# The router of a two-layer mixture kernel: kern products first, copies dropped, three of eight x pairs loaded transposed

## The reference, cut to what matters

```python
h = gelu(gelu(embedding @ W0 + b0) @ W1 + b1)
att = softmax(h @ W2 + b2)                                  # 32 x 8
agg_w = einsum('bk,koi->boi', att, weight[..., 0])
out = einsum('boi,bih->boh', agg_w, x) + (att @ bias_k)[:, :, None]
logits = einsum('bsh,he->bse', out, gate_w)
topv, topi = top_k(logits, 2); w = softmax(topv)
x = x + einsum('bsh,eho,bse->bso', out, expert_w, w_e)
```

## Time and profile before

| | us |
|---|---|
| runs, median of three (lowest, highest) | 869.05 (866.9, 869.88) |
| the profiled execution, its time | 863.12 |
| its span, first to last instruction | 861.3 |
| PE busy (x4356) | 824.4, 96% |
| DVE busy | 407.4, 47% |
| ACT busy | 229.6, 27% |
| POOL busy | 107.4, 12% |

### The profile page before, as it was taken

The page is one execution under the profiler, slowest core; times in us unless marked ns, Lnnn a source line. Parts: engine busy times, 40 slices in busy tenths (PEclk is TensorE's granted clock), DMA queues, the critical chain, the costliest instruction groups (busy, mean ns, idle before and its releaser), DMA issues.

```text
span 861.3 us, 13429 instructions
## 1 busy us (share of the span) xinstructions
PE 824.4 (96%) x4356; PEld 680.6 (79%) x4357; DVE 407.4 (47%) x944; ACT 229.6 (27%) x359; POOL 107.4 (12%) x145
## 2 busy tenths in 40 slices
PE   6999679999999999999999999999999999999986
PEld 5565468888888888888888888888898889889863
DVE  1577753142333313333133051466666656656597
ACT  2565333142333313333243151310010010001100
POOL 1122221101101001111011112121112111100000
PEclk9999879999999999999999999999999999999999
DMA  8744359655372724727246243575644654630048
GB/s 265 311 170 151 120 210 404 267 179 200 120 257 73 285 92 134 244 78 287 85 157 226 92 167 117 194 242 133 153 105 106 157 127 97 141 78 24 1 127 263
DMA packets 60789, 142.98 MB, mean 166 GB/s; under 512 B 6832, under 2 KB 23488, under 8 KB 60608
## 3 DMA queue, kind: packets, MB, share of 16 engines
q1 hardware_dynamic: 40096, 87.12, 31.1%
q0 software_dynamic: 9968, 36.19, 14.5%
q10 hardware_dynamic: 10704, 19.41, 6.0%
HBM read 94.45 MB, written 39.85 MB: 156 GB/s over the span
## 4 chain that ended last, share of the span: by engine, by line
PE 83%; DVE 6%; DMA 4%; issue 3%; ACT 1%; SPq 1%; DVEq 0%; ACTq 0%; POOL 0%; POOLq 0%
PE bank L1269 62%; PE bank L1308 6%; PE bank L1260 4%; PE bank L1317 4%; PE bank L1169 2%; PE bank L1371 1%; PE bank L1137 1%; DVE work L1111 1%; PE bank L1148 1%; DMA work<-in_expert_w 1%; PE bank L1192 1%; PE bank L1217 1%; DVE rank_all L812 1%; DMA work<-y_scratch,pos_c 1%; DMA x1p<-res 1%
## 5 line engine op out<-in xcount | busy, mean ns | idle before, releaser
L1269 PE MATMUL bank<-weights,l_hi 128*128 128x512 f32 x1696 | 523.6, 390 | 0.0
L1269 PEld LDWEIGHTS bank<-weights,l_hi 128*128 128x128 f32 x1696 | 319.2, 188 | 64.7
L1269 PE MATMUL bank<-weights,l_lo 128*128 128x512 f32 x848 | 335.8, 396 | 1.2 <-DVE l_lo L900 1.1
L1269 PEld LDWEIGHTS bank<-weights,l_lo 128*128 128x128 f32 x848 | 159.7, 188 | 33.4 <-issue 2.3
L900 DVE TENSOR_TENSOR l_lo<-bank,l_hi 128x512 fp32r<-128x512 f32 x37 | 25.6, 693 | 183.6 <-ACT l_hi L679 183.6
L932 DVE TENSOR_TENSOR weights<-work,weights 128x1024 fp32r<-128x1024 f32 x64 | 76.2, 1223 | 50.4 <-ACT weights L690 49.8
L690 ACT ACTIVATE weights<-work 128x1024 fp32r<-128x1024 f32 x64 | 65.1, 1054 | 41.3 <-DMA work<-in_expert_w 23.2
L537 POOL DMA_INDIRECT work<-c_scratch,idx x37 | 41.5, 1122 | 193.6 <-PE bank L1260 192.5
L730 ACT ACTIVATE l_hi<-work 128x512 fp32r<-128x512 f32 x32 | 18.4, 623 | 158.2 <-PE bank L1269 157.5
L1308 PE MATMUL bank<-conv_sb,x1p 128*128 128x128 f32 x512 | 59.8, 275 | 0.4 <-DMA x1p<-res 0.4
L1308 PEld LDWEIGHTS bank<-conv_sb,x1p 128*128 128x128 f32 x512 | 58.8, 192 | 0.7 <-DMA x1p<-res 0.7
(11 more groups left out here) (178 smaller groups left out, 577.2 us busy)
## 6 DMA issues: line engine op xcount, KB each, us to landing
work<-in_expert_w SPq DMA_DIRECT2D x68, 512.0 KB, 6.3
y_scratch<-work ACTq DMA_DIRECT2D x74, 256.0 KB, 2.1
res<-in_x SPq DMA_DIRECT2D x16, 512.0 KB, 15.4
c_scratch<-work SPq DMA_DIRECT2D x16, 512.0 KB, 3.0
out<-work SPq DMA_DIRECT2D x16, 512.0 KB, 4.3
res<-in_x_ph SPq DMA_DIRECT2D x14, 512.0 KB, 5.6
x1p<-res SPq DMA_DIRECT2D x112, 64.0 KB, 4.7
y_scratch<-ca SPq DMA_DIRECT2D x7, 512.0 KB, 9.3
```

What stands on the lines that cost most here:

```text
L1269: mm = pe.matmul(to[:, :], a[:, k, :], b[:, k, cols * HALF:(cols + 1) * HALF], start=(k == 0 and n == 0), stop=(k == HC - 1 and n == 2))
```

## The change

Four edits, all ahead of the expert products:

- PE's kern products (L1217) move ahead of the three small products and of the last two turns of pair 0. The small products use `bank[5]`. ACT and DVE make their copies to `bd` first.
- DVE's rounds are written out instead of looped. Four small copies go (L812, L813, L846, L854): ranks, indices, largest values and counts are written where they are used later.
- The pairs 3, 5 and 7 (`LOADED`) aren't turned by PE. SP loads them a second time from `x_t`, a transposed copy of x that the host lays out, 1 MB a pair, into `xt_pair`. PE waits for the load in `gate_products`, and for the plain x in `mix`.
- ACT's `round0` follows `ROUNDS`: chunks 1 and 2 at the end of round 1, 4 and 5 at the end of round 3, 6 in round 4, 7 in round 5, none in rounds 6 and 7. SP's loads of the chunks keep their place.

```diff
+LOADED = [3, 5, 7]
+ROUNDS = [[0], [1, 2], [3], [4, 5], [6], [7], [], []]
...
             for it in range(NT // 2):
+                if it + 2 in LOADED:
+
+                    sp.wait_ge(s_g, (it + 1) * QUAD)
+                    n = LOADED.index(it + 2)
+                    sp.dma_start(row(it % 2 * 2, 2), x_t[tile_rows(n), :]).then_inc(s_xtl, 16)
                 for j in range(2):
 
                     sp.wait_ge(s_cev[j], 2 * (it + 1))
...
             def take_turned(it, n):
 
-                act.wait_ge(s_t, it * 4 + n + 1)
+                if it in LOADED:
+                    return
+                act.wait_ge(s_t, turned(it) * 4 + n + 1)
...
-            for n in range(4):
+            for n in range(2):
                 take_turned(0, n)
-            act.wait_ge(s_pe0, 7)
+            act.wait_ge(s_pe0, 5)
             for g in range(QUAD // 2, QUAD):
                 for b in range(2):
                     act.activation(*block(g, b), ACT.Copy).then_inc(s_bda, 1)
+            for n in range(2, 4):
+                take_turned(0, n)
...
                 take_c0(it, 1)
-                round0(it)
+                for k in ROUNDS[it]:
+                    round0(k)
...
                 wait_apart(dve, s_rk, it * 2 + 2)
-                ch.link(dve.tensor_reduce(rk4[:, :], rk4v, AX.X, ALU.add))
-                ch.add(dve.tensor_copy(rank_all[:, bass.ds(it * 4, 4)], rk4[:, :]))
-                ch.add(dve.tensor_copy(ix_all[:, bass.ds(it * 4, 4)], ixf[:, :]))
-                ch.link(dve.scalar_tensor_tensor(pos_s[:, :], ixf[:, :], float(N), rk4[:, :], ALU.mult, ALU.add))
+                four = slice(it * 4, it * 4 + 4)
+                ch.link(dve.tensor_reduce(rank_all[:, four], rk4v, AX.X, ALU.add))
+                ch.link(dve.scalar_tensor_tensor(pos_s[:, :], ix_all[:, four], float(N), rank_all[:, four], ALU.mult, ALU.add))
...
-                ch.add(dve.tensor_copy(mx_all[:, bass.ds(it * 2, 2), :], mx[:, :, 0:2]))
...
-                ch.add(dve.tensor_copy(pre[:, 0, :], acc[:, :]))
...
-                pe.wait_ge(s_xt, (it + 1) * 4)
+                if it in LOADED:
+                    pe.wait_ge(s_xtl, 16 * (LOADED.index(it) + 1))
+                else:
+                    pe.wait_ge(s_xt, (turned(it) + 1) * 4)
...
+                if h == 0 and it in LOADED:
+                    pe.wait_ge(s_x[t], 16)
...
-            pe.wait_ge(s_const, 16)
-            pe.wait_ge(s_gred, 1)
-            pe.matmul(bank[2][:, 0:E], ones, gl[:, :], start=True, stop=True)
-            pe.matmul(bank[3][0:B, 0:CH], c("emb"), c("cw"), start=True, stop=True).then_inc(s_pe0, 1)
-            pe.wait_ge(s_attx, 1)
-            pe.matmul(bank[7][:, B * K8:2 * B * K8], c("ones", B), attx[:, :, :].rearrange("p n k -> p (n k)"),
-                      start=True, stop=True).then_inc(s_pe0, 1)
-            turn_x(0, 2)
-            turn_x(0, 3)
             pe.wait_ge(s_kern, 16 * QUAD)
             pe.wait_ge(s_att, 2)
-            pe.wait_ge(s_ctx0, 1)
...
             mm.then_inc(s_pe0, 1)
+            pe.wait_ge(s_const, 16)
+            pe.wait_ge(s_gred, 1)
+            pe.matmul(bank[5][:, 0:E], ones, gl[:, :], start=True, stop=True)
+            pe.matmul(bank[5][0:B, CH:2 * CH], c("emb"), c("cw"), start=True, stop=True).then_inc(s_pe0, 1)
+            pe.wait_ge(s_attx, 1)
+            pe.matmul(bank[7][:, B * K8:2 * B * K8], c("ones", B), attx[:, :, :].rearrange("p n k -> p (n k)"),
+                      start=True, stop=True).then_inc(s_pe0, 1)
+            turn_x(0, 2)
+            turn_x(0, 3)
```

More of the change, by code:

```diff
@@ L86, with build @@
 ROW_OF = np.arange(P).reshape(2 * CQ, CP).T.reshape(-1)
-def build(nc, x, kern, x_ph, consts_a, consts_b, expert_w, conv_w, down_w, lora_b, out):
+def build(nc, x, x_t, kern, x_ph, consts_a, consts_b, expert_w, conv_w, down_w, lora_b, out):
     ctx = ExitStack()
@@ L190, in build @@
         lg = sb("lg", [P, 2, E])
-        mx = sb("mx", [P, 2, 8])
         ix = sb("ix", [P, 2, 8], U32)
-        mx_all = sb("mx_all", [P, NT, 2])
-        ixf = sb("ixf", [P, 4])
+        mx_all = sb("mx_all", [P, NT, 8])
         oh = sb("oh", [P, 2, 2, E])
         msk = sb("msk", [P, 2, E])
-        pre = sb("pre", [P, 2, E])
-        acc = sb("acc", [P, E])
+        pre = sb("pre", [P, NT + 1, E])
         rk = sb("rk", [P, 2, 2, E])
-        rk4 = sb("rk4", [P, 4])
         pos_s = sb("pos_s", [P, 4], I32)
@@ L256, in build @@
         s_gred = sem("s_gred")
+        s_xtl = sem("s_xtl")
         s_rk = sem("s_rk")
@@ L365, in slots, with turned @@
                         body(g, e, odd, False)
+        def turned(it):
+            return it - sum(n < it for n in LOADED)
         def block(g, b):
@@ L523, in _ @@
             pool.memset(bd[:, :, :], 0.0).then_inc(s_init, 1)
-            pool.memset(acc[:, :], 0.0).then_inc(s_init, 1)
+            pool.memset(pre[:, 0, :], 0.0).then_inc(s_init, 1)
             pool.memset(acc2[:, :], 0.0).then_inc(s_init, 1)
@@ L620, in _ @@
             act.wait_ge(s_init, 5)
-            act.activation(warm[:, 0:1], acc[:, 0:1], ACT.Gelu)
+            act.activation(warm[:, 0:1], acc2[:, 0:1], ACT.Gelu)
             act.wait_ge(s_mlp, 16)
@@ L626, in _ @@
             act.activation(h1[:, :], bank[1][:, 0:B], ACT.Gelu, bias=c("b1")).then_inc(s_act0, 1)
-            act.activation(warm[:, 1:2], acc[:, 1:2], ACT.Exp)
+            act.activation(warm[:, 1:2], acc2[:, 1:2], ACT.Exp)
             act.wait_ge(s_sm, 1)
@@ L775, in _ @@
             dve.wait_ge(s_pe0, 5)
-            ch.add(dve.tensor_copy(gsum[:, :], bank[2][:, 0:E]))
-            dve.tensor_tensor(ctx0[:, :], bank[3][0:B, 0:CH], c("fside", B), ALU.add).then_inc(s_ctx0, 1)
+            for g in range(QUAD // 2):
+                for b in range(2):
+                    dve.tensor_copy(*block(g, b)).then_inc(s_bdv, 1)
             dve.wait_ge(s_pe0, 6)
+            ch.add(dve.tensor_copy(gsum[:, :], bank[5][:, 0:E]))
+            dve.tensor_tensor(ctx0[:, :], bank[5][0:B, CH:2 * CH], c("fside", B), ALU.add).then_inc(s_ctx0, 1)
+            dve.wait_ge(s_pe0, 7)
             ch.wait()
@@ L784, in _ @@
             dve.tensor_reduce(aggb[:, :], aggb_q, AX.X, ALU.add).then_inc(s_aggb, 1)
[L785 to L788, removed]
             dve.wait_ge(s_aggb, 1)
@@ L832, in one_hot @@
                     ins = dve.tensor_scalar(oh_hi[:, m, :], c("iota"), hi_f[:, m:m + 1],
-                                            c("tok")[:, bass.ds(it * 2 + m // 2, 1)], ALU.is_equal, ALU.mult)
+                                            c("tok")[:, it * 2 + m // 2:it * 2 + m // 2 + 1], ALU.is_equal, ALU.mult)
                 ins.then_inc(s_hot, 1)
@@ L839, in route @@
                 for j in range(2):
-                    n = ch.add(dve.scalar_tensor_tensor(lg[:, j, :], gsum[:, :], aggb[:, bass.ds(it * 2 + j, 1)],
+                    n = ch.add(dve.scalar_tensor_tensor(lg[:, j, :], gsum[:, :], aggb[:, it * 2 + j:it * 2 + j + 1],
                                                         bank[5][:, L_AT + j * E:L_AT + (j + 1) * E], ALU.mult, ALU.add))
-                wait_apart(dve, s_chA, ch.base + n)
+                ch.wait(n)
+                mx = mx_all[:, it * 2:it * 2 + 2, :]
                 for j in range(2):
@@ L849, in route @@
                 ch.wait()
-                ch.link(dve.tensor_copy(ixf[:, :].rearrange("p (j k) -> p j k", j=2), ix[:, :, 0:2]))
-                ch.link(dve.tensor_tensor(oh4, iota4, ixf[:, :].unsqueeze(2).to_broadcast([P, 4, E]), ALU.is_equal))
-                dve.wait_ge(s_m, it)
-                ch.add(dve.tensor_copy(pre[:, 0, :], acc[:, :]))
+                ixf = ix_all[:, it * 4:it * 4 + 4]
+                ch.link(dve.tensor_copy(ixf.rearrange("p (j k) -> p j k", j=2), ix[:, :, 0:2]))
+                ch.link(dve.tensor_tensor(oh4, iota4, ixf.unsqueeze(2).to_broadcast([P, 4, E]), ALU.is_equal))
+                if it > 0:
+                    dve.wait_ge(s_r, it)
                 ch.link(dve.tensor_tensor(msk[:, :, :], oh[:, :, 0, :], oh[:, :, 1, :], ALU.add))
-                ch.link(dve.tensor_tensor(pre[:, 1, :], pre[:, 0, :], msk[:, 0, :], ALU.add))
-                dve.tensor_tensor(acc[:, :], pre[:, 1, :], msk[:, 1, :], ALU.add).then_inc(s_m, 1)
-            LA = 20
+                ch.link(dve.tensor_tensor(pre[:, it * 2 + 1, :], pre[:, it * 2, :], msk[:, 0, :], ALU.add))
+                dve.tensor_tensor(pre[:, it * 2 + 2, :], pre[:, it * 2 + 1, :], msk[:, 1, :], ALU.add).then_inc(s_m, 1)
+                dve.wait_ge(s_m, it + 1)
             take_rows(0)
             take_gate(0)
[L863 to L870, removed]
+            ch = Chain(dve, s_chA)
+            route(ch, 0)
+            for it in range(1, NT // 2):
                 take_rows(it)
-                place(ch, it - 1, it)
+                place(ch, it - 1, it, it == 1)
                 route(ch, it)
[L874 to L880, removed]
+            place(ch, NT // 2 - 1, None)
```

(11 more changed lines are left out.)

## The result

| | us | ratio to the kernel before, 95% interval |
|---|---|---|
| before, median of 20 runs | 867.4 (863.9 to 869.9) | |
| changed, median of 20 runs | 871.5 (867.7 to 875.7) | 1.0051 (1.0036 to 1.0066) |
| forecast | 867.9 (863.0 to 872.5) | no change |

The change makes the kernel slower by 4.1 us, 3 to 6 by the interval. I had called no change the likeliest and faster likelier than slower. That 871.5 still lies between 863.0 and 872.5 is luck of the base: the forecast is 1.2 us under the three runs that I had (median 869.05), and 1.2 us under the median of twenty would be 866.2. The profiled execution of the changed kernel took 872.7 us, its span is 870.9. The profiled execution before, 863.1, was faster than each of the twenty runs (lowest 863.9).

The account below looks back on a forecast made before the run. The prediction took the chain in the rounds as two thirds PE, one third a DVE chain behind POOL. Rounds and tail at -3.7 plus the start gave -1.2 us: 867.9 us, range 863 to 872.5.

Parts of the forecast that it names:

- Start: Ahead of the rounds: kern products begin at 13.1 when kern has landed, first gate products end at 27.6, +2.5 us.
- The hold passes on: DVE in the rounds: with L812 dropped, POOL's step holds L814 instead; round 1 gains only 0.1 us.
- Rival B: POOL holds less of DVE than thought, L814 and casts run beside L530: -4.5 to -6, 863.8 us; chance 0.27.
- Round 2: Round without turns but with two POOL steps holding DVE's small instructions ahead of the logits: 10.7 us against 9.5.
- Rival D: PE's idle 3 us in round 2 drops the clock to the 1.2 GHz level: +1.8, 870.9 us; chance 0.13.
- Rounds 4 and 5: Late weight chunks, with a load landing of 4.2 us, hold up ACT: 20.1 us together against 19.0.
- Round 3 and all rounds with turns: Round 3: POOL's single step ends early and holds nothing, 3.6 to the logits plus 5.3 of PE, 8.9 us.
- Round 6: No turns, and POOL late enough to miss DVE's `place`: logits at 3.1 plus 4.4 of PE, 7.5 us.
- Transposed loads are free: SP's 1 MB loads, issued over a round ahead of use, cost nothing; bounds 0 and 1 us.
- Rival E: Turned pairs shorten nothing, since DVE's chain sets all rounds: +1.6, 870.7 us; chance 0.07.
- Rival C: Weight loads come later still, with a landing of 6.3 us, delaying PE in round 5: +3.0, 872.1 us; chance 0.13.
- Behind L883: Expert products and after, untouched by the change: a length differing by over a us would prove the prediction wrong.

Follow-up runs that it names:

- a3: Kernel before with the new start alone (kern products first): 871.8 us, ratio 1.0053.
- c3: a4 with no pair loaded transposed, leaving the dropped copies and DVE's written-out rounds: 865.8 us, ratio 0.9982.
- a4: Changed kernel with the old start and one weight chunk per round; transposed pairs and dropped copies kept: 862.4 us, ratio 0.9940.
- b3: a1 with chunks 1 and 2 still rounded together but no later chunk right behind its load's issue: 864.9 us, ratio 0.9972.
- a1: Changed kernel with the old start, small products and last turns ahead of the kern products again: 867.3 us, ratio 1.0002.
- a2: Changed kernel with one weight chunk rounded per round, as before: 866.8 us, ratio 0.9986.
- b1: a4 with one wait more, so POOL's step on a chunk starts behind DVE's one-hots of the next round: 860.2 us, ratio 0.9907.
- b2: Kernel before with only the added wait that puts POOL's step behind DVE's one-hots: 863.2 us, ratio 0.9943.
- b4: Changed kernel with the four kern loads issued ahead of x and the rest of the constants: 871.0 us, ratio 1.0031.
- c2: c1 with six pairs, 2 to 7, loaded transposed: 852.8 us, ratio 0.9833.
- c1: b1 with SP's load of a weight chunk moved behind the c0 stores of the round before its use: 856.5 us, ratio 0.9872.
- c4: Kernel before, unchanged, profiled a second time: one execution, 868.9 us.

## Why the prediction was wrong

The parts in the medians, each from a ratio times 867.4: start +4.6 (a3), dropped copies -1.6 (c3), three transposed pairs -3.6 (a4 less c3), double step +2.8 (b3 less a4), late chunks +2.6 (a1 less b3). Sum +4.8; measured +4.4 (0.51%). Each part is uncertain by 1 to 2 us. The forecast, -1.2, had the mechanisms of all five. It failed in sizes, and nearly all the errors went one way: the start is 2.1 us of the 5.6 missed, the clock in round 2 some 1.6.

- *Start, +2.5 forecast, +4.6 measured.* The failed term is the landing of kern, 13.1. In the three profiles in which PE stood ready for it, PE was released at 13.98 (a3), 14.18 (a2) and 16.00, in a4 and c3, with the old start, at 16.51 and 17.37. I had taken the end of the low DMA rate for the landing. No view prints the landing where PE comes later, but the trace has the updates of the semaphore `s_kern`: the last comes at 14.3 in the kernel before, and between 13.4 and 17.3, median 15.4, in all thirteen profiles with this order of loads. So 14 was too low even as an upper bound, and the better bound was in the rows: L1217 began at 16.11, and none showed that its load had come earlier. From the products on the sum held: 14.7 us to T0 in all three.
- *The hold passes on.* Right: L826 takes 2.09 us beside POOL, L828 2.27 behind it. The Trainium skill, "SBUF — State Buffer", "Who interferes with whom", is borne out in the cases seen here: held are L826 and L869 with two SBUF inputs (up to 2.32 us) and L828, a tensor_scalar of four int32; not held are the reduction L825 (0.19 us beside POOL) and, in b1, L851 with an input in PSUM (0.22 each). b2 shows the converse. Rival B is refuted.
- *Round 2, 10.7.* Right with the clock up (10.53 in a1). Rival D, given 0.13, is what the changed kernel did: 12.19 with the clock down, and again 12.14 in b3 and 13.55 in b4, three of four profiles with the double step. It was not an alternative to the forecast but part of it; I should have added its chance times its price, 1.6 us by the mean of these four. In the changed kernel's tail the clock fell once more, at 102, and the first four mixing products took 3.52 us. There the forecast had 12.7 and 14.1 came; in b4, with the clock up at that point, it was 12.4.
- *Rounds 4 and 5, 20.1.* Right in sum (19.87); the load's landing of 4.2 is the median that the after profile shows for L398. The split was not: the POOL step of chunk 5 met the one-hots, so round 4 took 10.2, and this gave chunk 6 time to come, at T0+2.2 and not 4.1, so round 5 took 9.65 and not 11.7.
- *Round 3 and all rounds with turns, 8.9.* Too low: 9.17, in b2 six times with nothing held ahead of the logits. They come at T0+3.5 there, where I had 3.6; from them to the next T0 are 5.65 us and not 5.3, and in this stretch PE does have a hole: the third turn, at 50.94, waits for ACT's copy of the second. *Round 6,* 7.5: 7.88, since chunk 7's POOL step held L869, which I had put past the route.
- *Transposed loads are free.* Right, three (no wait in the after profile's list) and six (c2). Rival E is refuted: rounds without turns take 8.42 in a4 against 9.35 in c3, and 7.43 in c1 against 9.17 with turns.
- *Rival C* (chunks later still) did not come: landings were 4.2. Its 872.1 us is near the 871.5 measured, by chance.
- *Behind L883.* I had written that over a us there would prove me wrong. It was 2.2, but c4 has 3.8 between two executions of the kernel before. And the profile that all my rows are from was a fast one twice, here and by 2.1 us in round 0; one profile more would have shown both.

## What to carry to other kernels

Work that stands ahead of a product in program order may be the cover for its load: before moving the product forward, find a row that shows the load landed, and if there is none, let the upper bound reach to the time at which the product ran. A small vector instruction that takes as long as a GpSimd one beside it is held by it; dropping the instruction passes the hold to the next, while moving the GpSimd step puts the hold where the vector engine has time to spare (5 us for one wait, b2). Before such a move look at what waits for that step: in b1 it held back stores, and 3.7 us of the gain came only with c1. Where an edit leaves TensorE idle (2.8 us here), price the products behind the gap at both clock levels, and put the second into the sum. Profile the kernel before twice: what differs between two executions of the same code is no target.

## What the runs showed of the hardware

- Beside two POOL steps of 2.34 us in a row DVE got one small instruction done per step: L826, begun 0.3 us after the first, ended with it (2.09 us for 0.16), and L828 then took 2.27 us and ended with the second (0.17 alone).
- An idle gap of 2.8 us on PE let the granted clock fall in the changed kernel, b3 and b4 and not in a1. The gate products of pair 0 took 1.9 us in every profile, as at the 1.2 GHz level, against 1.05 in later rounds, although 7 us of kern products stood ahead of them.
- Four loads of 64 KB into 8 partitions each, issued at 3.6 to 4.7 us, landed between 13.4 and 17.3 us, while the two loads of 512 KB issued at 2.2 and 3.1 landed at 5.6 to 6.3 and 10.6 to 13.7. Executions of the same order of loads differ by 4 us in this.
